# Off-diagonal maxima moved behind the tasks, a new task table, masks in row halves, and a copy moved to GpSimd

## The reference

```python
# x (8, 1024, 256) fp32; 16 heads of 16; HIDDEN = 768
xn = _layernorm(x)
qkv = xn @ W_attn + b_attn            # q, k, v: (8, 16, 1024, 16)
# q, k rotated by tables over the HEAD index n: cos/sin(n * theta)
att = softmax(where(causal, q k^T / 4, -inf))
s = (att v) @ W_proj + b_proj
h = silu(xn @ wg.T) * (xn @ wu.T)     # wg, wu, wd: int32 / 127
g = silu(h @ wd.T)
out = x + s * g
```

## Time and profile before

| | |
|---|---|
| median of 3 runs | 1412.45 us (1411.94 to 1413.13) |
| the profiled execution | 1412.94 us, span 1411.2 us |
| TensorE busy | 1333.2 us (94%) |
| VectorE busy | 1007.6 us (71%) |
| ScalarE busy | 983.3 us (70%) |
| GpSimd busy | 626.5 us (44%) |
| mean granted clock of TensorE | 0.979 of 2.4 GHz |

### The profile page before, as it was taken

One profiled execution on the slowest core, in us unless ns is written; L12 is line 12 of the kernel. 1 busy time (PEld: TensorE's weight loads), 2 busy tenths in 40 slices (PEclk: granted clock), 3 DMA queues, 4 the chain that ended last, 5 costly groups with the idle time before them and its releaser, 6 DMA issues.

```text
span 1411.2 us, 28890 instructions
## 1 busy us (share of the span) xinstructions
PE 1333.2 (94%) x10631; PEld 549.7 (39%) x10631; DVE 1007.6 (71%) x1930; ACT 983.3 (70%) x2186; POOL 626.5 (44%) x751
## 2 busy tenths in 40 slices
PE   3899999999999999999999999999999999999986
PEld 1223433434344433434334343443334443343333
DVE  6688777777777767787777777777777777767711
ACT  2157677786767777676777767777776777778673
POOL 4117332573426444464435734265343643344352
PEclk9679999999999999999999999999999999999998
DMA  2620112202041020401213020410204002120101
GB/s 79 171 76 2 48 30 96 56 1 92 2 120 32 2 91 17 128 10 36 57 53 99 2 79 14 120 33 2 91 16 121 17 10 83 37 85 2 31 2 46
DMA packets 56769, 73.58 MB, mean 52 GB/s; under 512 B 9010, under 2 KB 34994, under 8 KB 56628
## 3 DMA queue, kind: packets, MB, share of 16 engines
q1 hardware_dynamic: 56052, 70.95, 16.7%
q10 hardware_dynamic: 576, 0.79, 0.3%
HBM read 46.01 MB, written 25.17 MB: 50 GB/s over the span
## 4 chain that ended last, share of the span: by engine, by line
PE 71%; ACT 11%; DVE 9%; issue 4%; POOL 3%; DMA 1%; ACTq 0%; POOLq 0%; SPq 0%; DVEq 0%
PE ring L730 24%; PE acc L722 15%; PE st L672 11%; PE ring L696 7%; PE ring L704 5%; ACT pexp L896 4%; PE ring L817 4%; DVE mx_a L1030 3%; ACT th L942 2%; PE ring L792 2%; DVE ga L1092 1%; ACT mT L964 1%; ACT parts L932 1%; PE ring L826 1%; PE ring L807 1%
## 5 line engine op out<-in xcount | busy, mean ns | idle before, releaser
L896 ACT ACTIVATE pexp<-st 128x512 f32<-128x512 f32 (+3 forms) x1536 | 659.4, 494 | 82.5 <-PE st L672 78.6
L1030 DVE TENSOR_REDUCE mx_a<-ring 128x1 f32<-128x512 f32 (+3 forms) x896 | 534.5, 646 | 134.3 <-PE ring L704 74.8
L1250 POOL TENSOR_SCALAR_AFFINE_SELECT pexp<-pexp 128x512 f32<-128x512 f32 x256 | 162.5, 635 | 510.3 <-ACT pexp L896 510.3
L722 PE MATMUL acc<-pexp,v_pad 128*17 128x512 f32 (+3 forms) x3072 | 324.3, 494 | 15.6 <-POOL pexp L1250 12.4
L672 PE MATMUL st<-q_st,k_st 50*128 50x512 f16 (+3 forms) x1536 | 299.8, 335 | 17.6 <-ACT pexp L896 16.1
L696 PE MATMUL ring<-k_st,q_st 48*128 48x512 f16 (+3 forms) x1536 | 270.0, 333 | 9.7 <-DMA k_st<-parts_scratch 6.0
L1030 DVE TENSOR_REDUCE mx_b<-ring 128x1 f32<-128x384 f32 (+3 forms) x384 | 212.8, 596 | 53.2 <-PE ring L704 50.4
L672 PEld LDWEIGHTS st<-q_st,k_st 50*128 50x128 f16 x1536 | 85.0, 93 | 409.1 <-ACT pexp L896 268.3
L1281 POOL TENSOR_TENSOR hf<-ga,ups 128x512 f32<-128x512 f32 x96 | 121.8, 1269 | 68.6 <-ACT ups L947 57.1
L1286 POOL TENSOR_TENSOR hT<-hf,hT 128x512 f16<-128x512 f32 x96 | 111.0, 1157 | 91.3 <-ACT hT L915 91.3
L704 PE MATMUL ring<-tri,identb 128*128 128x128 bf16 (+1 forms) x768 | 126.1, 247 | 0.0
(11 more groups left out here) (113 smaller groups left out, 1554.3 us busy)
## 6 DMA issues: line engine op xcount, KB each, us to landing
parts_scratch<-parts SPq DMA_DIRECT2D x32, 512.0 KB, 2.8
q_st<-parts_scratch SPq DMA_DIRECT2D x192, 64.0 KB, 2.4
k_st<-parts_scratch SPq DMA_DIRECT2D x180, 64.0 KB, 2.2
xn<-in_x SPq DMA_DIRECT2D x8, 1024.0 KB, 5.9
xo<-in_x SPq DMA_DIRECT2D x32, 256.0 KB, 2.8
out<-xo SPq DMA_DIRECT2D x32, 256.0 KB, 2.2
q_st<-mT SPq DMA_DIRECT2D x128, 4.0 KB
pexp<-in_w_attn SPq DMA_DIRECT2D x1, 768.0 KB, 4.5
```

What stands on the lines that cost most here:

```text
L722: mm = nc.tensor.matmul(acc[32 * j:32 * j + D + 1, CH - w:CH], v_pad[:, kb, GH * g + j, :], pexp[:, GH * (n % NSET) + j, 0:w], start=kb == ...
L896: nc.scalar.activation(pexp[:, GH * (n % NSET) + j, 0:w], st[:, (GH * n + j) % NST, 0:w], ACT.Exp, scale=1.0 / (QK_SCALE * np.sqrt(D))).th ...
L1030: nc.vector.reduce_max(dst, ring[:, b, 0:len(heads) * w].rearrange("p (s w) -> p s w", w=w), AX.X)\
L1250: nc.gpsimd.affine_select(out=t, in_=t, compare_op=ALU.is_ge, fill=0.0, base=0, pattern=[[0, GH], [1, P]], channel_multiplier=-1).then_inc ...
```

## The change

- TensorE makes the maxima of a slot's second item, with no mask, at the end of half 0, behind the tasks, and no longer in half 1 behind the scores. VectorE's code follows.
- The mask on the diagonal maxima is added by four matmuls, 64 rows high, in place of two of 128: for each row half an identity of the upper 64 outputs with all 128 keys, then one of the lower 64 outputs with the last 64 keys. Constants for it are made by GpSimd, and a DMA on SyncE copies half of `tri`.
- HI is done by GpSimd, with the same lag.
- `TASKS` and `END_TASKS` are new.
- In the prologue SyncE and no longer ScalarE issues the six loads of k for group 1.

`BLOCKS`, `DIAG_ORDER`, `diag_count` and the tests in `values` are written differently and give the same numbers.

```diff
 TASKS = {
-    0: [("FT", 1), ("DN", 1, 2)],
-    1: [("DN", 1, 3)],
-    2: [("FT", 0), ("XC", 0)],
-    3: [("FP", 0)],
-    4: [("UPG", 0, 0), ("UPG", 0, 1)],
-    5: [("FP", 1)],
-    6: [("UPU", 0, 0)],
-    7: [("V", 0, 1), ("UPU", 0, 1), ("LNS", 0), ("LNS", 1), ("LNS", 2)],
-    8: [("V", 1, 0)],
-    9: [("MT", 1), ("YT", 3, 1), ("LNS", 3)],
-    10: [("UPG", 0, 2), ("UPU", 0, 2), ("LNR",)],
-    11: [("V", 1, 1)],
-    12: [("UPG", 0, 3), ("UPU", 0, 3), ("XC", 1)],
-    13: [("YT", 0, 0), ("UPG", 0, 4), ("LNA", 0)],
-    14: [("UPU", 0, 4)],
-    15: [("FT", 2), ("FT", 3)],
-    16: [("UPG", 0, 5), ("UPU", 0, 5), ("LNA", 2)],
-    17: [("YT", 0, 1), ("LNA", 6)],
-    18: [("YT", 1, 0), ("LNA", 3)],
-    19: [("LNA", 1)],
-    20: [("TX", 1, 0), ("DN", 0, 0), ("LNA", 4), ("LNA", 5), ("LNA", 7)],
-    21: [("MT", 2), ("TX", 1, 1)],
-    22: [("TX", 0, 1), ("DN", 0, 1)],
-    23: [("QK", 0, 0, 1), ("QK", 0, 1, 1)],
-    24: [("TX", 0, 0), ("FP", 2)],
-    25: [("QK", 0, 0, 0)],
-    26: [("QK", 0, 1, 0)],
-    27: [("DN", 0, 2)],
-    28: [("FP", 3)],
-    29: [("UPG", 1, 0)],
-    30: [("DN", 0, 3)],
-    31: [("UPU", 1, 0)],
-    32: [("QK", 1, 0, 1)],
-    33: [("MT", 3), ("UPG", 1, 1)],
-    34: [("UPU", 1, 1)],
-    35: [("UPG", 1, 2), ("UPU", 1, 2)],
-    36: [("YT", 1, 1), ("V", 0, 0)],
-    37: [("YT", 2, 0), ("UPG", 1, 3)],
-    38: [("UPU", 1, 3)],
-    39: [("UPG", 1, 4), ("UPU", 1, 4)],
-    40: [("QK", 1, 1, 0), ("UPG", 1, 5)],
-    41: [("YT", 2, 1), ("UPU", 1, 5)],
-    42: [("YT", 3, 0), ("QK", 1, 0, 0)],
-    44: [("QK", 1, 1, 1)],
-    45: [("MT", 0)],
+    0: [("DN", 1, 2), ("FT", 0)],
+    1: [("UPG", 0, 0)],
+    2: [("DN", 1, 3)],
+    3: [("FP", 0), ("XC", 0)],
+    4: [("UPU", 0, 0), ("XC", 1)],
+    5: [("UPG", 0, 1), ("FT", 1), ("LNS", 0)],
+    6: [("LNS", 1), ("V", 0, 1), ("LNS", 2), ("FP", 1)],
+    7: [("UPG", 0, 2)],
+    8: [("LNS", 3), ("UPU", 0, 1)],
+    9: [("MT", 1), ("YT", 0, 0)],
+    11: [("UPU", 0, 2), ("V", 1, 1), ("LNR",), ("YT", 3, 1)],
+    12: [("UPG", 0, 3), ("V", 1, 0)],
+    13: [("UPG", 0, 4)],
+    14: [("FT", 2), ("LNA", 6), ("LNA", 7)],
+    15: [("UPU", 0, 3), ("LNA", 1)],
+    16: [("UPU", 0, 4)],
+    17: [("UPG", 0, 5), ("FT", 3)],
+    18: [("LNA", 2), ("LNA", 0), ("YT", 1, 0)],
+    19: [("LNA", 4), ("UPU", 0, 5)],
+    20: [("UPG", 1, 0), ("UPG", 1, 1)],
+    21: [("MT", 2), ("YT", 0, 1), ("LNA", 3), ("LNA", 5)],
+    22: [("TX", 1, 0), ("FP", 2)],
+    23: [("TX", 0, 0), ("TX", 0, 1), ("TX", 1, 1), ("DN", 0, 0)],
+    24: [("QK", 0, 0, 0), ("DN", 0, 1)],
+    25: [("DN", 0, 2)],
+    26: [("QK", 0, 1, 0), ("QK", 0, 1, 1), ("QK", 0, 0, 1), ("DN", 0, 3)],
+    27: [("UPU", 1, 0)],
+    28: [("UPU", 1, 1)],
+    29: [("UPG", 1, 2), ("FP", 3)],
+    30: [("YT", 1, 1)],
+    31: [("QK", 1, 1, 1), ("UPG", 1, 3)],
+    32: [("UPU", 1, 2)],
+    33: [("MT", 3), ("YT", 2, 0)],
+    35: [("V", 0, 0)],
+    36: [("UPU", 1, 3)],
+    37: [("QK", 1, 0, 0), ("UPG", 1, 4)],
+    39: [("UPU", 1, 4)],
+    41: [("UPG", 1, 5), ("UPU", 1, 5)],
+    42: [("YT", 3, 0)],
+    43: [("QK", 1, 1, 0)],
+    45: [("QK", 1, 0, 1), ("MT", 0), ("YT", 2, 1)],
 ...
+END_FROM = 28
 END_TASKS = {
+    28: [("UPU", 1, 1)],
+    29: [("UPG", 1, 2), ("FP", 3)],
+    30: [("YT", 1, 1)],
+    31: [("QK", 1, 1, 1), ("UPG", 1, 3)],
+    32: [("UPU", 1, 2)],
+    33: [("MT", 3), ("YT", 2, 0)],
+    35: [("V", 0, 0)],
+    36: [("UPU", 1, 3)],
+    37: [("QK", 1, 0, 0), ("UPG", 1, 4)],
+    39: [("UPU", 1, 4)],
+    41: [("UPG", 1, 5), ("UPU", 1, 5)],
+    42: [("YT", 3, 0)],
+    43: [("QK", 1, 1, 0)],
+    45: [("QK", 1, 0, 1), ("MT", 0), ("YT", 2, 1)],
 ...
 LAG = {
-    "scalar": {"TX": 0, "QK": 0, "UPG": 0, "UPU": 0, "V": 0, "DN": 0, "FT": 0, "FP": 0, "MT": 0, "HI": 3},
+    "scalar": {"TX": 0, "QK": 0, "UPG": 0, "UPU": 0, "V": 0, "DN": 0, "FT": 0, "FP": 0, "MT": 0},
     "vector": {"TX": 0, "QK": 0, "UPG": 0, "DN": 0, "YT": 0, "LNS": 1, "BP": 0},
-    "gpsimd": {"LNR": 0, "LNA": 1, "XC": 1, "UPU": 2, "LO": 4, "FP": 2, "FP_G": 3, "FP_X": 4},
+    "gpsimd": {"LNR": 0, "LNA": 1, "XC": 1, "UPU": 2, "HI": 3, "LO": 4, "FP": 2, "FP_G": 3, "FP_X": 4},
     "sync": {"QK": 2, "MT": 1, "FP": 5},
 }
 ...
@@ -575,7 +576,7 @@
                     _, hf_, which, c = t
                     if t == [u for u in BY["QK"].seen[kind] if u[1:3] == (hf_, which)][-1]:
                         store_parts(kind, i, hf_, which)
-                        if hf_ == 0 and which == 1:
+                        if hf_ == 0 and t == [u for u in BY["QK"].seen[kind] if u[1] == 0][-1]:
                             for g in range(2):
                                 load_stacks(i + 1, g, 2 * i + 3)
                 if t[0] == "MT":
@@ -598,6 +599,8 @@
                 sp.dma_start(b_pr[:, :], b_proj.broadcast_to([P, C])).then_inc(w_in["rest"], 16)
                 sp.dma_start(w_pr[:, :, :], w_proj.rearrange("(k p) n -> p k n", p=P)).then_inc(w_in["proj"], 16)
+                sp.wait_ge(const_ready, 7)
+                sp.dma_start(tri[64:P, :, :], tri[0:64, :, :]).then_inc(tri_in, 16)
                 sp.wait_ge(b_turned, 1)
                 sp.dma_start(bias_dram, b_row[:, :]).then_inc(b_back, 16)
                 sp.wait_ge(b_back, 16)
@@ -608,6 +611,7 @@
                 sp.wait_ge(k_const, 1)
                 for g in range(2):
                     load_stack(sp, sp_stand, 0, g, 0, 1)
+                load_stack(sp, sp_stand, 0, 1, 1, 1)
                 sp.dma_start(w_raw["gate"], w_gate_t.rearrange("(k p) n -> p k n", p=P)).then_inc(w_in["gate"], 16)
                 sp.dma_start(w_raw["up"], w_up_t.rearrange("(k p) n -> p k n", p=P)).then_inc(w_in["up"], 16)
                 sp.dma_start(w_raw["down"], w_down_t.rearrange("(k p) n -> p k n", p=P)).then_inc(w_in["down"], 16)
@@ -699,11 +703,15 @@
                             mm.then_inc(ready, 1)
                 if half == 0:
                     n = len(heads)
-                    for a in range(2):
-                        b = bank(kind, t_ring, a)
-                        nc.tensor.matmul(ring[:, b, 0:n * w].rearrange("p (s w) -> p s w", s=n)[:, :, w - P:w],
-                                         identb[:, :], tri[:, 0:n, :], start=False, stop=True)\
-                            .then_inc(ring_ready[b], 1)
+                    for h in range(2):
+                        keys = P - 64 * h
+                        for a in range(2):
+                            b = bank(kind, t_ring, a)
+                            rows = slice(SIDE * a, SIDE * a + 64)
+                            mm = nc.tensor.matmul(ring[:, b, 0:n * w].rearrange("p (s w) -> p s w", s=n)[:, :, w - keys:w],
+                                                  ident64[rows, h, :], tri[rows, 0:n, 0:keys], start=False, stop=h == 1)
+                            if h == 1:
+                                mm.then_inc(ring_ready[b], 1)
             def values(i, g, n):
@@ -866,11 +875,13 @@
                     g, n = divmod(slot, STEPS)
                     for half in range(2):
                         scores(i, g, n, half)
-                        if has_max(kind, slot) and names_of(kind, ("MX", slot, half)):
-                            maxima(kind, i, slot, half)
                         if half == 0:
+                            if has_max(kind, slot):
+                                maxima(kind, i, slot, 0)
                             for t in tasks_at(kind, slot):
                                 task(kind, i, t)
+                            if has_max(kind, slot) and names_of(kind, ("MX", slot, 1)):
+                                maxima(kind, i, slot, 1)
                         elif slot > 0:
                             values(i, *divmod(slot - 1, STEPS))
                         elif kind != "first":
@@ -984,8 +990,7 @@
                         act.wait_ge(ones_ready, 4)
                     if t == ("QK", 1, 0, 0):
                         act.wait_ge(k_const, 1)
-                        for g in range(2):
-                            load_stack(act, act_stand, 0, g, 1, 1)
+                        load_stack(act, act_stand, 0, 0, 1, 1)
                     task("pro", 0, t)
             def body(kind, i):
@@ -1198,14 +1203,16 @@
             def body(kind, i):
                 for slot in range(SLOTS):
                     for half in range(2):
-                        if has_max(kind, slot) and names_of(kind, ("MX", slot, half)):
-                            max_take(kind, i, slot, half)
+                        if half == 0 and has_max(kind, slot):
+                            max_take(kind, i, slot, 0)
                         if half == 0 and slot + 1 < SLOTS:
                             for t in tasks_at(kind, slot + 1):
                                 if t[0] == "MT":
                                     split_maxima(kind, i, t)
                         for t in parts_at("vector", kind, slot, half):
                             task(kind, i, t)
```

(16 more changed lines are left out.)

52 lines of the change are left out of this document (25 added, 27 removed).

## The result

The changed kernel takes 1343.06 us, median of four runs (1341.15 to 1344.42), against 1412.44 (1411.94 to 1413.13) beside it on the same chip: ratio 0.9507, 95% interval 0.9492 to 0.9522. That is 69 us faster. I had forecast 1392 with 1374 to 1414: the sign was right, the size and the range were wrong.

The account below looks back on a forecast made before the run. TensorE, busy 94% of the span, was taken as the bound. Arriving work -13, new waits +13, old waits -9, chain -9, copies -4 + 4, prologue -3 made -21, from 1411.2 to 1390, stated as 1392; range 1374 to 1414.

Parts of the forecast that it names:

- Two kinds matter: Of TensorE's 13 us of waits a batch, two matter: for exponentials in slots without tasks, and for GpSimd's mask of pexp.
- What of it arrives: TensorE's 21.7 us less work counts only where TensorE is last ready: 60% let through, 13 us, with waits reckoned against it.
- New empty slots: Slots 10, 34, 38, 40 and 44, left without tasks: new TensorE waits of 1.6 us a batch, +13 us.
- Old empty slots and the chain: Slots 19 and 43 get tasks, 9 us less waits; GpSimd's chain of 14 operations moves to slot 11, 9 us less.
- Masks and change-overs: On TensorE, masks in row halves save 14 us, fewer mode change-overs 7.6 us; 60% of each arrives, 13 us.
- Copy on GpSimd: 96 copies of h's high part leave ScalarE for GpSimd: 4 us credited, 4 us charged for masks held up.
- Order of the second maxima: Second scores stand behind second maxima: exponentials start 0.22 us later, felt only in empty slots and charged there.
- Prologue: Six loads of k go from ScalarE to SyncE: first maxima 2.8 us earlier, near 47.2; -3 us.
- (b): With the copies gone ScalarE is never last; 3 more us of waits go in each batch: 1368; chance 0.07.
- (c): VectorE's ring and the exponentials take all of TensorE's gain, old empty slots' 9 us included: 1414, say 1412; chance 0.08.
- (d): Short mask matmuls on TensorE cost their start, not their columns: 1415; chance 0.05.
- (e): GpSimd's copy before the mask makes values wait 1.2 us each; four such waits a batch make 1430; chance 0.12.

## Why the prediction was wrong, by its own steps

- **What failed: "Two kinds matter" of TensorE's 13 us of waits, and with it "What of it arrives".** I named the chain, and the exponentials of an empty slot, and let all other waits of the old table stand. Those others were 9.4 us of the 13, and the new tables take 4.5 of them away, 36 us over eight batches. By my terms the tables gave +13 - 9 - 9 = -5 us (and, with the half masks, 60% of 7.6 more); alone they measured -45.
- **New empty slots: +13 forecast.** Their waits came as I priced them: 1.6 a batch forecast, 1.5 measured. But two of them (34 and 38) had waited 1.0 in the old table already, and I charged the whole as new: it is 0.5, 4 us.
- **Old empty slots and the chain: right.** Slots 19 and 43: 1.1 a batch forecast, 1.1 measured. Chain: -9 forecast; of its 1.28 a batch 0.07 is left. Moved alone in the old table it gains nothing, so it needs what the new table puts around it. I took the margin as 0.4; it is 0.9.
- **Masks and change-overs.** Work 21.7 forecast, 23 measured (3.0 in each middle batch, 3.7 and 1.5 in the first and the last). 60% of it was to arrive, 13 us; measured +11 when the masks are undone. I had the reason right too: what doesn't arrive is mostly in the empty slots.
- **Copy on GpSimd.** -4 + 4 forecast. In the old table it gives -3.6, my credit, with no charge seen; in the new one -13. The price was 0.55 against 0.61 measured, 6 us more of GpSimd's time in all, and the values wait less for GpSimd than before (6.5 us against 12.4). That the same work of ScalarE is worth three times as much in the new table was in no term: I summed parts as if they were independent.
- **Order of the second maxima**: neutral forecast, +0.8 measured. **Prologue**: -3 forecast, first maxima 46.1 where I said 47.2, first scores 4.2 us earlier (75.7); with the same prologue they start at 75.7 to 78.8 in other profiled runs, so 1 to 4.
- **Rivals.** (b), "faster still" at 1368, named the sign of the error, at two thirds of its size, and for another reason (the copies). (c), nothing comes back, fell with the result. (d), short matmuls, fell: full-height masks cost 11 us more. In the prediction I took the 60 cycles that the Trainium skill, "TensorEngine Tiling (Array Packing)", section "Instruction Overhead", puts on each matmul as a price on top of the columns. The trace disagrees with that reading, at 0.028 us a pair of 64 columns and 0.058 a pair of 128. (e) fell: values wait for GpSimd 6.5 us in all.
- **The books.** Tables -45 (put in first), half masks -11, copy -13, order -1 (each taken out last) make -70, against -69 measured, with the prologue's 1 to 4 in none of them. The sum depends on the order: taken out of the changed kernel the tables are worth 60, put in alone the copy 4 and the masks 5.

**What stays open.** Of the table's 45 us, the groups of slots (a middle batch times eight, which makes 49) give the chain 10, the old empty slots 9, less 6 that the new ones cost, and 8 to the two slots behind MT; the run with MT beside UPU shows that mechanism and its size, 0.9 a slot. The rest, some 28 us by the last two lines of the table of groups, is spread over many slots. For slots 5 and 29 a run shows that UPG in the slot before brings 0.2 to 0.3 back, but its removal from slots 16 and 40 of the old table did not help slots 17 and 41. What the new tables leave in slots 5 and 17 goes with another step order, but comes back in other slots. No single cause is shown for these 28 us.

## What to carry to other kernels

When a table of tasks is replaced, read the waits of TensorE by start-to-start in every slot of the old one, not only in the slots that the argument is about; what is left over is the largest unknown of the sum and belongs in the range. A long eviction (MT, 1.0 us) wants a slot in which ScalarE has nothing else, and a serial chain on GpSimd wants long tasks of TensorE behind it and no product ahead of it: moved alone, the same chain made the kernel slower by 9 us. Look at the granted clock before a difference is put down to waits: at the end of waits of 2.2 to 2.6 us it halved for some microseconds, and of a loss of 31 us that was 13. Cuts of work pay in full only where that engine ends last: half of TensorE's 23 us came back as waits, and 60 us of ScalarE's copies were worth 4 us in one table and 13 in the other.

## What the runs showed of the hardware

- Matmuls of 64 columns in two row halves start 0.028 us apart as a pair, half of what 128 columns take (0.058): at this size no start cost shows in the rate.
- A cast of 128x512 from fp32 to fp16 on GpSimd takes 612 ns, about as long as ScalarE's copy did (647), and half of a two-input operation there (1161).
- TensorE's granted clock can fall inside a batch: in three runs in which TensorE waited 2.2 to 2.6 us for a mask once a batch, it fell to 0.50 (1.2 GHz) within about 1 us of the wait's end, for 3.4 or 6.8 us, in six, six and three batches of seven. In the kernel before, with waits of 1.2 us there, no middle batch has a fall.
- The small dependent operations of the chain on GpSimd, 0.20 us each, start 0.38 us apart; the other half is the wait of each for the one before ("0.18 <-POOL").
